# Router gate as extra columns of the shared expert's first matmul, routing one iteration later

## The reference

```
h = layernorm(x) * (1 + ca) + sa
x = x + ga * (tanh(h B^T) C^T + D * h)                    # state width 256
h = layernorm(x) * (1 + cb) + sb
scores = sigmoid(h gate_w^T)                              # 8 experts
idx = top 2 of (scores + router_bias);  w = scores[idx] / their sum
y = sum over the two of w_e * (silu(h W1_e) * (h W3_e)) W2_e     # 352 inner
x = x + gb * (y + (silu(h sw1) * (h sw3)) sw2)            # shared: 704 inner
```

## Time and profile before

| | |
|---|---|
| median of 3 runs | 624.21 us (622.14 to 624.47) |
| the profiled execution | 623.48 us, span 621.8 us |
| mean granted TensorE clock | 0.968 of full speed |
| TensorE busy | 568.3 us, 91% of the span |
| VectorE, ScalarE, GpSimd busy | 324.3, 177.7, 239.4 us |
| first iteration with a gate (3) begins | 63.6 us |
| expert stage begins on TensorE | 253.4 us |

### The profile page before, as it was taken

The page is one execution under the profiler, slowest core; times in us unless marked ns, Lnnn a source line. Parts: engine busy times, 40 slices in busy tenths (PEclk is TensorE's granted clock), DMA queues, the critical chain, the costliest instruction groups (busy, mean ns, idle before and its releaser), DMA issues.

```text
span 621.8 us, 11647 instructions
## 1 busy us (share of the span) xinstructions
PE 568.3 (91%) x3304; PEld 510.5 (82%) x3305; DVE 324.3 (52%) x647; ACT 177.7 (29%) x331; POOL 239.4 (39%) x199
## 2 busy tenths in 40 slices
PE   5766889999999887599989999989999999999995
PEld 2445779889889776599988999979999999999994
DVE  1577878788787868432231222222222225767766
ACT  1220533433442431122232222222232232222220
POOL 1386647647745742160035600173270003232231
PEclk9977989999999998699999999999999999999999
DMA  8970546312222235666256752369562225455443
GB/s 314 370 255 1 203 183 247 130 67 101 101 85 84 103 136 202 215 209 230 68 200 214 251 212 67 87 213 360 218 211 84 84 69 164 142 171 167 135 136 118
DMA packets 37560, 102.72 MB, mean 165 GB/s; under 512 B 4256, under 2 KB 4256, under 8 KB 36640
## 3 DMA queue, kind: packets, MB, share of 16 engines
q1 hardware_dynamic: 27952, 53.65, 25.0%
q0 software_dynamic: 9152, 47.98, 21.7%
q10 hardware_dynamic: 432, 0.79, 0.3%
HBM read 71.73 MB, written 30.67 MB: 165 GB/s over the span
## 4 chain that ended last, share of the span: by engine, by line
PE 77%; DVE 11%; issue 3%; DMA 3%; POOL 3%; ACT 1%; SPq 1%; DVEq 0%; POOLq 0%; ACTq 0%
PE bank L768 13%; PE bank L770 12%; PE bank L769 12%; PE bank L782 7%; PE bank L784 7%; PE bank L783 7%; PE bank L754 5%; PE bank L789 3%; PE bank L730 3%; PE bank L719 2%; PE bank L721 2%; PE bank L720 2%; PE bank L840 2%; POOL wlo L461 2%; DMA whi<-w_all 1%
## 5 line engine op out<-in xcount | busy, mean ns | idle before, releaser
L768 PE MATMUL bank<-whi,thi 128*128 x416 | 140.1, 337 | 5.1 <-POOL wlo L461 5.1
L770 PE MATMUL bank<-whi,tlo 128*128 x416 | 135.2, 325 | 0.0
L769 PE MATMUL bank<-wlo,thi 128*128 x416 | 135.1, 325 | 0.0
L782 PE MATMUL bank<-whi,gth 128*128 (+1 forms) x204 | 81.8, 401 | 4.8 <-DVE wlo L1130 1.9
L768 PEld LDWEIGHTS bank<-whi,thi 128*128 128x128 f32 x416 | 79.0, 190 | 6.3 <-issue 6.3
L461 POOL TENSOR_TENSOR wlo<-raw,whi 128x1408 f32 (+3 forms) x21 | 69.0, 3306 | 36.9 <-DMA whi<-w_all 36.8
L1360 DVE TENSOR_TENSOR gbuf<-s,bank 128x352 f32<-128x352 f32 x52 | 27.0, 519 | 104.3 <-ACT s L698 104.1
L784 PE MATMUL bank<-whi,gtl 128*128 (+1 forms) x204 | 80.9, 397 | 0.0
L783 PE MATMUL bank<-wlo,gth 128*128 (+1 forms) x204 | 80.7, 396 | 0.0
L1364 DVE TENSOR_TENSOR gtl<-bank,gth 128x384 fp32r<-128x384 f32 x52 | 29.0, 557 | 97.8 <-ACT gth L702 92.1
L769 PEld LDWEIGHTS bank<-wlo,thi 128*128 128x128 f32 x416 | 79.3, 191 | 0.0
(11 more groups left out here) (183 smaller groups left out, 1055.7 us busy)
## 6 DMA issues: line engine op xcount, KB each, us to landing
raw<-w_all POOLq DMA_DIRECT2D x7, 2176.0 KB
whi<-w_all POOLq DMA_DIRECT2D x14, 704.0 KB
h<-xs_rows SPq DMA_DIRECT2D x36, 256.0 KB
ys_rows<-tmpa SPq DMA_DIRECT2D x36, 256.0 KB, 2.0
whi<-w_all POOLq DMA_DIRECT2D x7, 768.0 KB, 13.1
x_all<-wmod SPq DMA_DIRECT2D x4, 1024.0 KB, 9.0
x_all<-x SPq DMA_DIRECT2D x4, 1024.0 KB, 9.0
hs_rows<-h SPq DMA_DIRECT2D x8, 512.0 KB, 2.8
```

The source lines that it names most:

```text
L768: pe.matmul(dst, xh[:, j, a], wh, start=(m == 0), stop=False)
L769: pe.matmul(dst, xh[:, j, a], wl, start=False, stop=False)
L770: mm = pe.matmul(dst, xl[:, j, a], wh, start=False, stop=(m == KD - 1))
L782: pe.matmul(dst, gth[:, a], wh, start=(m == 0), stop=False)
```

## The change

The 8 gate columns of a weight row are put in front of the 352 columns of shared expert A's first matrix, in `whi` and `wlo`, split into high and low part as the other weights are. A's up for half 0 then has 360 columns and leaves the gate's logits in the first 8 columns of bank 2. The separate gate, `xtf` and their waits remain only for the last pair. ScalarE copies the logits of each tile to `lg` behind the Silu, and makes the Sigmoid of the pair at the end of the iteration, behind `gth` of tile 1. The routing of pair p (all twelve steps, `ranks`, the load of `hrow` and the scatter) moves from iteration p+3 to p+4; in an iteration steps 0 to 6 keep their places, 7 to 11 come after everything else. `ranks` stands behind the last `turn_g`. In iteration 10 pair 6 and pair 7 are both routed: pair 6 first, pair 7 with its own gate and ranks in bank 6. `UPA = UP + E` and `SH = KD * E`; `whi` and `wlo` grow by SH columns, and every other weight address moves by SH. The diff, cut to its core:

```diff
             return lo - lag >= 0 and hi - lag < NP
+        def routes(lo, hi):
+            return lo - 4 >= 0 and hi - 4 < NP - 1
...
             def body(it, lo, hi):
-                if live(3, lo, hi):
-                    p = it - 3
+                if routes(lo, hi):
+                    p = it - 4
                     left = value(sp, p * 64)
                     sp.wait_ge(s_nat, p * 16 + 16)
-                    if is_last(lo):
-                        sp.wait_ge(s_xd, NP)
-                    elif lo > 3:
+                    if lo > 4:
                         sp.wait_ge(s_scat, left)
-                    sp.dma_start(hrow[is_last(lo)], hs[bass.ds(p * 2 * P, 2 * P), :].rearrange("(b p) d -> p b d", p=P)
-                                 ).then_inc(s_hrow[is_last(lo)], 16)
+                    sp.dma_start(hrow[0], hs[bass.ds(p * 2 * P, 2 * P), :].rearrange("(b p) d -> p b d", p=P)
+                                 ).then_inc(s_hrow[0], 16)
+                if is_last(lo):
+                    sp.wait_ge(s_nat, NP * 16)
+                    sp.wait_ge(s_xd, NP)
+                    sp.dma_start(hrow[1], hs[(NP - 1) * 2 * P:NP * 2 * P, :].rearrange("(b p) d -> p b d", p=P)
+                                 ).then_inc(s_hrow[1], 16)
                 if live(2, lo, hi):
...
-                def scatter():
-                    p = it - 3
-                    landed, known = value(pool, p * 16 + 16), value(pool, p * KR + KR)
+                def scatter(p, last):
+                    landed, known = 16 if last else value(pool, p * 16 + 16), value(pool, p * KR + KR)
                     pool.wait_ge(s_fold, 1)
-                    pool.wait_ge(s_hrow[is_last(lo)], 16 if is_last(lo) else landed)
+                    pool.wait_ge(s_hrow[last], landed)
                     pool.wait_ge(s_rt, known)
...
                             pool.indirect_dma_start(
-                                xs[:, :], bass.IndirectOffsetOnAxis(ap=idx4[is_last(lo)][:, 2 * j + k:2 * j + k + 1],
-                                                              axis=0),
-                                hrow[is_last(lo)][:, j, :], None).then_inc(s_scat, 16)
-                if live(3, lo, hi) and is_last(lo):
-                    scatter()
-                if live(3, lo, hi) and not is_last(lo):
-                    scatter()
+                                xs[:, :], bass.IndirectOffsetOnAxis(ap=idx4[last][:, 2 * j + k:2 * j + k + 1], axis=0),
+                                hrow[last][:, j, :], None).then_inc(s_scat, 16)
+                if is_last(lo):
+                    scatter(it - 4, 0)
+                    scatter(it - 3, 1)
+                if routes(lo, hi) and not is_last(lo):
+                    scatter(it - 4, 0)
                 if lo in (NP, NP + 1):
...
                     act.wait_ge(q["A", "g"], p * 2 + j)
-                act.activation(s1[:, :], bank[2][:, 0:F], ACT.Silu).then_inc(q["A", "silu"], 1)
+                act.activation(s1[:, :], bank[2][:, E:E + F], ACT.Silu).then_inc(q["A", "silu"], 1)
+                if not is_last(lo):
+                    act.activation(lg[:, bass.ds(p * 2 + j, 1), :].rearrange("p a e -> p (a e)"), bank[2][:, 0:E],
+                                   ACT.Copy).then_inc(s_lg, 1)
                 act.wait_ge(q["A", "gt"], n)
...
                         act.wait_ge(q["A", "up"], p * 2)
-                        act.wait_ge(s_gate, p)
-                    else:
-                        act.wait_ge(s_gb, 1)
                     for j in range(2):
                         act.activation(xah[:, j, :], bank[4 + j][:, :], ACT.Copy).then_inc(q["A", "xhi"], 1)
-                        act.activation(xtf[:, j, :], bank[4 + j][:, :], ACT.Copy).then_inc(s_xtf, 1)
-                    act.wait_ge(s_gate, p + 1)
-                    act.activation(sc[:, bass.ds(p * 2, 2), :],
-                                   bank[7][:, 0:2 * E].rearrange("p (b e) -> p b e", b=2),
-                                   ACT.Sigmoid).then_inc(s_sc, 1)
+                        if is_last(lo):
+                            act.activation(xtf[:, j, :], bank[4 + j][:, :], ACT.Copy).then_inc(s_xtf, 1)
+                    if is_last(lo):
+                        act.wait_ge(s_gate, 1)
+                        act.activation(sc[:, bass.ds(p * 2, 2), :],
+                                       bank[6][:, 0:2 * E].rearrange("p (b e) -> p b e", b=2),
+                                       ACT.Sigmoid).then_inc(s_sc, 1)
                     if lo == 3:
...
                     hidden(it - 3, 1, lo)
+                    if not is_last(lo):
+                        p = it - 3
+                        act.wait_ge(s_lg, p * 2 + 2)
+                        act.activation(sc[:, bass.ds(p * 2, 2), :], lg[:, bass.ds(p * 2, 2), :],
+                                       ACT.Sigmoid).then_inc(s_sc, 1)
...
             modulation(4)
+            act.wait_ge(l_gate, 32)
+            act.activation(whi_a[:, :, 0:E], gw[:, :, :], ACT.Copy).then_inc(s_gwh, 1)
             body(2, 2, 2)
...
                     for h in range(2):
-                        w = off + (m * UP + h * F)
-                        wh, wl = whi[:, bass.ds(w, F)], wlo[:, bass.ds(w, F)]
-                        dst = bank[2 + h][:, 0:F]
+                        if sec == "A":
+                            w, n = m * UPA + h * (E + F), F + (1 - h) * E
+                        else:
+                            w, n = off + (SH + m * UP + h * F), F
+                        wh, wl = whi[:, bass.ds(w, n)], wlo[:, bass.ds(w, n)]
+                        dst = bank[2 + h][:, 0:n]
                         pe.matmul(dst, xh[:, j, a], wh, start=(m == 0), stop=False)
...
                         pe.wait_ge(q["A", "g"], (it - 4) * 2 + 2)
+                        pe.wait_ge(s_lg, (it - 4) * 2 + 2)
                     for j in range(2):
...
+                def ranks(p, to):
+                    pe.wait_ge(s_rt, p * KR + KM)
+                    at_, all_ = 2 * E, 4 * E
+                    pe.matmul(to[:, at_:at_ + 2 * E], tri_b[:, :], mask[:, :, :], start=True, stop=False)
+                    pe.matmul(to[:, at_ + E:at_ + 2 * E], ones_b[:, :], mask[:, 0, :], start=False, stop=True)
+                    pe.matmul(to[:, all_:all_ + E], ones_b[:, :], mask[:, 0, :], start=True, stop=False)
+                    pe.matmul(to[:, all_:all_ + E], ones_b[:, :], mask[:, 1, :],
+                              start=False, stop=True).then_inc(s_rank, 1)
                 if is_last(lo):
                     last_tile()
-                if live(3, lo, hi):
-                    p = it - 3
-                    pe.wait_ge(s_xtf, p * 2 + 2)
-                    if lo > 3:
-                        pe.wait_ge(s_sc, p)
-                        pe.wait_ge(s_rt, (it - 4) * KR + KB)
+                    ranks(it - 4, bank[7])
+                    pe.wait_ge(s_xtf, 2)
+                    pe.wait_ge(s_tanh, NP * 2)
                     for j in range(2):
                         for k in range(KD):
-                            mm = pe.matmul(bank[7][:, j * E:(j + 1) * E], xtf[:, j, k * P:(k + 1) * P],
+                            mm = pe.matmul(bank[6][:, j * E:(j + 1) * E], xtf[:, j, k * P:(k + 1) * P],
                                            gw[:, k, :], start=(k == 0), stop=(k == KD - 1))
                     mm.then_inc(s_gate, 1)
+                if live(3, lo, hi):
                     if lo == hi == 3:
                         pe.wait_ge(w_ready, NW - 1)
-                if live(3, lo, hi):
+                        pe.wait_ge(s_gwl, 1)
                     if live(1, lo, hi):
...
                         pe.wait_ge(q["A", "g"], (it - 3) * 2)
+                        pe.wait_ge(s_lg, (it - 3) * 2)
                     up("A", it - 3, 0, 0)
...
                     last_tile()
-                def ranks():
-                    pe.wait_ge(s_rt, (it - 3) * KR + KM)
-                    at_, all_ = 2 * E, 4 * E
-                    pe.matmul(bank[7][:, at_:at_ + 2 * E], tri_b[:, :], mask[:, :, :], start=True, stop=False)
-                    pe.matmul(bank[7][:, at_ + E:at_ + 2 * E], ones_b[:, :], mask[:, 0, :], start=False, stop=True)
-                    pe.matmul(bank[7][:, all_:all_ + E], ones_b[:, :], mask[:, 0, :], start=True, stop=False)
-                    pe.matmul(bank[7][:, all_:all_ + E], ones_b[:, :], mask[:, 1, :],
-                              start=False, stop=True).then_inc(s_rank, 1)
                 if is_last(lo):
-                    ranks()
+                    ranks(it - 3, bank[6])
                 if live(3, lo, hi):
-                    pe.wait_ge(s_xtf, (it - 3) * 2 + 2)
+                    if is_last(lo):
+                        pe.wait_ge(s_xtf, 2)
+                    else:
+                        pe.wait_ge(q["A", "xhi"], (it - 3) * 2 + 2)
                     pe.wait_ge(q["A", "g"], (it - 3) * 2 + 1)
...
                     turn_g(bank[5]).then_inc(q["A", "gt"], 1)
```

(30 more changed lines are left out.)

45 lines of the change are left out of this document (28 added, 17 removed).

## The result

The changed kernel takes 626.30 us (median of 7 runs, 625.34 to 628.66); the kernel before, on the same chip, 624.02 (622.14 to 624.70). The ratio of the runs is 1.0056, 95% interval 1.0041 to 1.0071, so the kernel is slower, just past the 0.5% that the prediction set for no change. The medians alone lie 2.3 us apart here (0.37%) and 3.4 us on another chip (`e8_changed_again`). The forecast was 623.6, 0.6 us better than before: the time is inside the wide range of 618.5 to 627.5, outside the forecast's own 622 to 625, and the sign is wrong.

A forecast was written before the change was run, and what follows sets the result against it. A second cycle through VectorE and GpSimd, not TensorE alone, was taken to bound the loop. Terms -0.6 -1.55 +0 +0.84 +0.7 = -0.6 us gave 622.9 profiled, 623.6 as median; own range 622 to 625, wide range 618.5 to 627.5.

The forecast's parts named there:

- iteration 9: GpSimd's low part of the next weights still blocks `sel`; product and `turn_g` come later: cost 0.84 us.
- iteration 10: Two pairs routed, last row table 0.15 later, doubled scatter: cost 0.15 to 1.8 us, taken as 0.7.
- cover: End of first stage: 1 to 4 us between GpSimd's last scatter issue and the padding rows' issue and landing.
- The cycle through VectorE and GpSimd: Loop turn, iterations 5 to 8: freed 1.6 us becomes TensorE's wait for `low_a` of tile 0; turn 22.7, gain 0.
- slack of 0.74: Loop turn: room between `low_a` of tile 0 and TensorE's down of tile 0, 0.89 less about 0.15 us.
- delay of 0.84: Loop turn: route steps 7 to 11 in a row behind `low_a` start the scatter 0.84 us later.
- Rival (1): TensorE bounds everywhere: iterations 4 to 9 give 1.6 us each, with iteration 3 about 10: 614 us; chance 0.07.
- Iteration 4: No scatter ahead of `with_d`, so only TensorE's own work counts: gain 1.55 us.
- Iteration 3: No route; down of tile 0 waits for the weights' low part until 85.26: gain 0.2 to 0.88, taken 0.6.
- Rival (2): `sel` in iteration 9 slips through, 2.7 us better, or loop turns give 0.5 to 0.9 each: 618 to 621; chance 0.20.
- rival (4): Slower at the end alone: pads and first expert's rows wait for doubled scatter, 2 to 4 us: 625.5 to 627.5; chance 0.13.
- rival (3): Iterations 5 to 8: GpSimd's addition catches early `sel`, a turn loses 0.7 to 1.5 us: 626.5 to 629.5; chance 0.10.

The follow-up runs named there:

- e8_changed_again: The changed kernel itself, unedited, run and profiled again on another chip: 627.14 us, ratio 1.0057 to the kernel before.
- e1_interleave: The changed kernel with route steps 7 to 11 back between the other VectorE work and `ranks` back ahead of down of tile 0: 621.53 us, ratio 0.9967.
- b1_steps_in_row: The kernel before with route steps 7 to 11 in a row behind `low_a`, its gate left alone: 625.56 us, ratio 1.0039.
- c1_interleave_low: The changed kernel with the edits of `e1_interleave` and `e3_low_moved` together: 617.24 us, ratio 0.9900.
- e3_low_moved: The changed kernel with GpSimd's three low weight pieces moved, one each to iterations 4, 8 and 9: 620.06 us, ratio 0.9934.
- e4_idx_own: The changed kernel with an index buffer of its own for the last pair but one, so step 11 need not wait for the scatter: 625.74 us, ratio 1.0031.
- e2_scatter_lag: The changed kernel with the scatter put behind `rs1` of the next iteration, route steps left in a row: 624.20 us, ratio 1.0012.

## Why the prediction was wrong, point by point

Two steps of the prediction failed. It priced iteration 9 at 0.84, the delay of `turn_g`, and left out how long TensorE would then stand and what its clock does behind it: 2.75 and 1.41 us measured. And it priced iteration 10 at 0.7, with steps of the last pair done ahead of the weight piece and with "cover" for the padding rows: 2.47 and 2.86 us measured.

- **The cycle through VectorE and GpSimd**: right, and the main result. The slack of 0.74 and the delay of 0.84 gave 22.7 a turn, measured 22.63 to 22.70, TensorE's wait 1.60 to 1.63. That it fits to 0.05 us is partly luck, since two small errors cancel: from `turn_g` to the scatter it takes 3.56 us for 2.50, so the delay is 1.06, and from the scatter to `rs2` done 14.31 for 14.52, so the slack was about 0.95. `e1_interleave` and `b1_steps_in_row` show it from both sides. Rival (1), TensorE bounds everywhere, falls.
- **Iteration 4**: right, -1.60 for -1.55.
- **Iteration 3**: the mechanism is right, down of tile 0 begins at 84.41 and not at 85.26 behind `wlo` as said; what became of it was decided by the clock, from -1.92 to nothing (the lines at 84.41 and 84.77 above).
- **Iteration 9**: the delay of `turn_g` is right (0.83 in `b1_steps_in_row`). The step that failed is the one after it: I priced only how much later `turn_g` comes, and did not add that TensorE, without the gate, would reach it 1.8 us earlier and so stand for 1.01 + 0.8 + 1.8 = 3.6 us. That time is no loss in itself, but behind the pause of 3.58 us the clock fell, and behind 1.01 and 1.83 at the same place it did not. The length of the pause alone doesn't decide it: the clock also fell behind 2.74 (`e1_interleave`), 2.42 (`c1_interleave_low`) and 1.93 us (before, iteration 3, 85.26 in the earlier trace rows), and stayed up once behind 3.25. The Trainium skill (TensorE: Matmul & The Clock Gate, Part 1) says that the chip lowers the array's clock by how busy it has lately been, and that the moment varies from run to run; the two executions agree (24.14 and 22.80). Rival (2), that `sel` slips through, did not happen: `sel` came 0.36 us behind the start of the weight piece, near the margin of 0.4. With the piece out of the way iteration 9 takes 17.77 (`e3_low_moved`), 4.5 below my sum's 22.2, where the rival had 2.7.
- **Iteration 10**: the term of 0.7 was too small, 2.5 to 2.9 measured. Two things were mis-sized or missed. The missed one, 0.92 of it in the first execution, is the wait of step 11 for the landing of the scatter before: I went through the waits of GpSimd and SP on `s_scat` but not VectorE's, though the last pair's `sel` is queued behind it. So none of the last pair's steps was done when the weight piece ended, where I had counted on one or two and on 0.15 us: the piece ended 0.86 later in the iteration, as said, and the mask came 0.92 later. Removing the wait alone gains nothing there, as `e4_idx_own` shows, since `sel` is then held by the piece, as it was before (3.72 us). The other is rival (4): I saw the 1 MB, but called the distance to the padding rows "cover". Being issued earlier was no cover. By the comparison above it cost 1.5 to 1.9 us, a little under the 2 us at which that rival began. That the time lies in the rival's 625.5 to 627.5 is luck in part, since iteration 9 put in 1.4 to 2.8 us of it.
- **Iterations 5 to 8 caught by GpSimd**, rival (3): no sign of it in the changed kernel; `e2_scatter_lag` shows the same kind of hold at another step once GpSimd is early.

The sum missed by 3.0 us of span in the first execution: 1.9 in iteration 9, 1.8 at the end, 0.5 in the expert stage, 0.2 in the loop, less 1.3 at the start. In the second it missed by 4.1: 0.6 in iteration 9, 2.2 at the end, 0.6 in the expert stage, 0.2 in the loop, and 0.6 at the start. The end is the part that both have; what iteration 9 and the start put in depends on where the clock falls. Why the expert stage takes 0.5 to 0.6 us longer is open.

## What to carry to other kernels

When work is taken off the engine that seems to bound a loop, look for the second cycle, and place the steps that moved by that cycle's order and not by convenience: here five steps of a microsecond in all decided whether 4 us were had or not. A wait that grows because an engine arrives earlier is not free on TensorE: ask how long it will stand in one piece, and look at the clock behind it in more than one execution. And where two holds end at the same time, remove both in one kernel before judging either. A piece of work that is moved out of one collision can make another, as in iteration 9 of `c1_interleave_low`: look at what stands beside its new place.

## What the runs showed of the hardware

A VectorE operation with a single tensor input was held too: `idx<-pos`, 128x4, takes 0.17 us in the open, 2.13 beside GpSimd's x_all addition (`e2_scatter_lag`) and 1.72 beside a weight piece, ending with it. I had counted only two-input operations as exposed. The Trainium skill (SBUF — State Buffer, "SBUF: two separate sides") names two-input operations and those in a two-port mode; whether this one runs in such a mode no row here shows. GpSimd's next piece in a row of two did not let VectorE in between (`sel` 6.01 us beside 6.34 for two), while GpSimd's issuing of the scatters held neither `ahead` (0.29 us at 225.90 in the changed kernel) nor `ra` (0.19 at 228.59). One row does not fit: in `e4_idx_own` `sel` starts 0.44 us ahead of the weight piece, beside the last of the four issues, and still is held until the piece ends.
